# Layer 0 context attention: value products of all eight head pairs in one batch of four, in two PSUM banks

## The chip, the cores and the metric
The kernel is a four-layer network (a perceiver-like stack of cross attention, self attention and feed-forward blocks) written out by hand for one core of one Trainium2 chip. The metric is the device time of one execution in microseconds. Engines are named by their part: TensorE (PE in the rows, PEld for its weight loads), VectorE (DVE), ScalarE (ACT), GpSimd (POOL) and SyncE (SP), which issues the DMAs here.

## The reference, cut to what matters
Only the cross attention of layer 0 is touched. The input x has 128 batches of 32 rows of 128; the context has 257 rows of 256 for each batch. There are 16 heads of 64, and one learned null key and value beside the 257 of the context.

```python
def _L0_xattn_ref(x, context, Wq, Wkv, null_kv, Wout, ln_scale, ln_bias):
    HEADS, DH = 16, 64
    q = _split_heads(jnp.einsum('bnd,df->bnf', x, Wq)) * DH ** (-0.5)
    k, v = jnp.split(jnp.einsum('bmc,cf->bmf', context, Wkv), 2, axis=-1)
    ...                      # split into heads, the null key and value put in front
    attn = jax.nn.softmax(jnp.einsum('bhid,bhjd->bhij', q, k), axis=-1)
    out = jnp.einsum('bhij,bhjd->bhid', attn, v)
    out = jnp.einsum('bnf,fd->bnd', out.transpose(0, 2, 1, 3).reshape(b, -1, 1024), Wout)
    ...                      # layer norm with ln_scale and ln_bias
```

## The kernel before, in words
The kernel never forms keys and values. It multiplies the queries by the key weights (so that they stand in the 256 context channels), takes scores against the raw context, multiplies the probabilities by the raw context, and only then applies the value weights and the output weights.

The stage is `context_attention` (L3673). It works on 128 batches. Four batches make a tile (32 tiles of 4 x 32 = 128 rows). All its work is written out in one order for each engine, and the engines meet through counting semaphores. In the step of one batch n, at position b % 4 = 0, 1, 2 or 3 of its tile m, TensorE does in this order:

- `scores` (L3897): 16 matmuls of 257 columns into the four banks psA. It waits for `q_ready`, which both engines give when they have copied the queries out of psA (on VectorE L4084, on ScalarE L4036).
- `context` of the batch before (L3918): 128 matmuls into the four banks psB. It waits, among other things, for the transposed probabilities (`turned`, L4128) and for `values_read`, the count of value copies out of psB, since it writes those banks again.
- `fill` (L3881): 16 matmuls that make, in psA, the queries of the batch four later. Their copies are what the next `scores` waits for.
- `head_values` (L3929), at positions 1 and 3 only: the value weights applied to the finished contexts (`ot`) of the tile before. One call does four of the eight head pairs: 32 matmuls (four pairs, two halves of the context channels, two heads of a pair) into the one bank psB[:, 1]. VectorE copies the bank to `vo` (L4098) at the end of its own step.
- `output` (L3940, L3941), at position 0 only: 9 matmuls of the output weights with `vo`, for the tile two back, into psB[:, 2].
- `heads` (L3872): 4 matmuls for the queries of the next tile, into psB[:, 0], copied by ScalarE (L4042).

VectorE's step is: two maxima over the scores (L4105) with small follow-ups, the sum of the exponentials (L4117), its reciprocal, the copies of two context banks (L4090) and of two query banks (L4084), the scaling (L4123), the transpose (L4128), and at positions 1 and 3 the value copy (L4098). ScalarE does the exponentials (L4022) and the other copies. The first tile has no value products (there is no tile before it); the last tile has no `fill` and no `heads`, and its own values are computed behind the loop, in two banks of psA (L3929, 64 matmuls in one run). Each step of SyncE fetches one batch of the context in rows, and every second one two batches of it transposed, each behind a semaphore of its own; POOL copies the tail columns (L3837) and spreads them once a tile (L3846).

Which banks hold values when is told by `values_before`: it gives the count of value copies that `context` at position b must find done.

Of the kernel before, what the change touches and what calls it, by code (L numbers as in the profile page):

```python
# [26 lines left out]
BT = P // S  # L27
# [3645 lines left out]
def context_attention(k, w, w256_dram, nv_dram, queries_loaded):  # L3673
# [17 lines left out]
    with ctx:  # L3691
# [24 lines left out]
        psB = ps("c_psB", [P, G, CHUNK])  # L3716
# [24 lines left out]
        ot_ready = {e: k.sem(f"c_ot_ready_{e}") for e in ("act", "dve")}  # L3741
# [12 lines left out]
        def values_before(m, b, first):  # L3754

            if first and b < BT + 2:
                return None
            return 2 * (m - 1) + (b % BT) // 2

        with nc.Block() as block:  # L3760
            @block.sync
# [106 lines left out]
            def _(pe):  # L3868
# [7 lines left out]
                def fill(banks, j):  # L3876

                    for half in range(2):
                        for a in range(2):
                            for e in range(2):  # L3880
                                mm = pe.matmul(banks[:, 2 * a + e, half * P:(half + 1) * P],  # L3881
                                               w["k"][e * DV:(e + 1) * DV, 2 * j + a, half * P:(half + 1) * P],
                                               qh[e * DV:(e + 1) * DV, 2 * j + a], start=True, stop=True)
                    mm.then_inc(q_in, 1)

                def scores(i, b, first, last):
                    n = i * NB + b
                    for e in ("act", "dve"):
                        pe.wait_ge(q_ready[e], fills_before(i, b, last))
                    if b % 2 == 0:  # L3890
                        pe.wait_ge(kc_loaded[b // 2 % 2], (i * 2 + b // 4 + 1) * 32)
                    if not (first and b == 0):
                        pe.wait_ge(exp_done, n * EX)
                    pe.nop(nofuse=True)
                    for r in range(G):
                        for half in range(2):
                            mm = pe.matmul(psA[:, r, 0:KEYS],  # L3897
                                           qt[:, b // BT, half * BT + b % BT, r * G:(r + 1) * G].rearrange("p h i -> p (h i)"),
                                           kc[:, b // 2 % 2, b % 2, half], start=(half == 0), stop=(half == 1))
                        if r % 2:  # L3900
                            mm.then_inc(scores_done, 1)

                def context(n, b, count, valued, heads_read, outs_read, opening=False):

                    pe.wait_ge(turned, n + 1)
                    pe.wait_ge(vc_loaded[b % 4], count * 64)
                    pe.wait_ge(heads_ready, heads_read)
                    if valued is not None:
                        pe.wait_ge(values_read, valued)
                    if outs_read is not None:  # L3910
                        pe.wait_ge(out_read, outs_read)
                    if not opening:
                        pe.wait_ge(ot_ready["dve"], n)
                    pe.nop(nofuse=True)
                    for half in range(2):
                        for t in range(KB):
                            for e in range(G):
                                mm = pe.matmul(psB[:, e, half * P:(half + 1) * P],  # L3918
                                               vc[e * S:(e + 1) * S, b % 4, t, half * P:(half + 1) * P],
                                               pt[e * S:(e + 1) * S, :, t], start=(t == 0), stop=(t == KB - 1))  # L3920
                    mm.then_inc(context_done, 1)

                def head_values(bank, s, j):

                    for a in range(4):
                        for half in range(2):
                            for e in range(2):
                                h = (4 * j + a) * 2 + e
                                mm = pe.matmul(bank[e * DV:(e + 1) * DV, a * P:(a + 1) * P], wv[:, half, h],  # L3929
                                               ot[:, s, half * G + h // G, h % G].rearrange("p b i -> p (b i)"),  # L3930
                                               start=(half == 0), stop=(half == 1))
                    mm.then_inc(values_in, 1)

                def output(m, s):
                    pe.wait_ge(values_read, (m + 1) * 2)
                    pe.wait_ge(lz_ready, m + 1)
                    pe.wait_ge(wn_loaded[s], (m - s) * 32 + 64)
                    pe.nop(nofuse=True)
                    for p in range(H16 // 2):
                        pe.matmul(psB[:, 2, 0:D], vo[:, p], wo[:, p], start=(p == 0), stop=False)  # L3940
                    pe.matmul(psB[:, 2, 0:D], lz[:, s].rearrange("p b i -> p (b i)"), wn[:, s], start=False, stop=True)\  # L3941
                        .then_inc(out_done, 1)

                def chunk(i, first, last):
                    for b in range(NB):
                        n = i * NB + b
                        m, s = i * 2 + b // BT, b // BT
                        scores(i, b, first, last)
                        if not (first and b == 0):
                            c = (b - 1) % NB  # L3950
                            context(n - 1, c, i * 2 + (b - 1) // 4 + 1,
                                    values_before(m, b, first),
                                    min(n + 2, FILLS - FIRST + 1) if last else n + 2,
                                    m - 1 if b % BT == 1 and not first else None, first and b == 1)
                        if not (last and s == 1):
                            pe.wait_ge(heads_ready, n + 2)
                            pe.wait_ge(exp_done, n * EX + G)
                            pe.nop(nofuse=True)
                            fill(psA, b % BT)
                        if not (first and b == 0):  # L3960
                            pe.wait_ge(ot_ready["act"], n)
                        if b % 2 and not (first and s == 0):
                            if b % BT == 1:
                                pe.wait_ge(ot_ready["dve"], n)
                            pe.nop(nofuse=True)
                            head_values(psB[:, 1], 1 - s, b % BT // 2)
                        if b % BT == 0 and not first:
                            pe.wait_ge(ot_ready["dve"], n)
                            output(m - 2, s)
                        if not (last and (s == 1 or b == BT - 1)):  # L3970
                            to = (b + 1) % BT
                            pe.nop(nofuse=True)
                            heads(psB[:, 0], i * 2 + (b + 1) // BT + 1, (2 * to, 2 * to + 1))
# [107 lines left out]
            def _(v):  # L4081
# [11 lines left out]
                def take_values(bank, f, m, j, opening=False):  # L4093

                    v.wait_ge(values_in, f + 1)
                    if j == 0 and not opening:
                        v.wait_ge(out_done, m)
                    v.tensor_copy(vo[:, 4 * j:4 * j + 4].rearrange("p a t -> p (a t)"), bank)\  # L4098
                        .then_inc(values_read, 1)
# [38 lines left out]
                def chunk(i, first, last):  # L4138
                    for b in range(NB):
                        n = i * NB + b  # L4140
                        m, s = i * 2 + b // BT, b // BT
                        maxima(i, b)
                        if b % BT == 0 and not (first and b == 0):
                            turn_tail(m - 1, 1 - s)
                        invert(n, b)
                        if not (first and b == 0):
                            take_contexts(n - 1, (b - 1) % NB)
                        if not (last and s == 1):
                            take_queries(psA, n + FIRST, 1 - s, b % BT)
                        scale_and_turn(n, b, first)  # L4150
                        if b % 2 and not (first and s == 0):
                            take_values(psB[:, 1], 2 * (m - 1) + b % BT // 2, m - 1, b % BT // 2, first)
                        if b % BT == 2 and not first:
                            count_out(m - 2)

# [468 lines left out]
```

## Time and profile before

| | |
|---|---|
| median of 3 runs | 4436.02 us (4431.32 to 4437.11) |
| the profiled execution, its own time | 4436.19 us |
| its span in the trace | 4434.4 us, 116039 instructions |
| mean granted TensorE clock | 0.925 of full speed |
| busy shares of the span | TensorE 84%, VectorE 64%, ScalarE 45%, GpSimd 18% |
| the stage in question | about 94 to 1451 us of the span |

The span begins with the first instruction and ends with the last. A row of the timeline gives the start of a run of equal instructions, its length, the engine, the line, what it writes and reads, the shape and the count; idle time before it stands in square brackets with what ended it. The times of TensorE rows are those of pipelined matmuls: neighbouring rows overlap a little, so distances between starts are what is to be read.

### The profile page before, as it was taken

What the parts mean: (1) busy time and instruction counts of PE and PEld (TensorE: products, weight loads), DVE (VectorE), ACT (ScalarE), POOL (GpSimd) and SP (SyncE); (2) the same over time, 40 slices, a digit from 0 to 9 for tenths busy, and PEclk for the clock granted to TensorE, in tenths of its full rate; (3) what the DMA queues carried; (4) which work ended last, traced back from release to release, by engine and by line L of the source; (5) the groups of instructions that cost most, each with busy time, mean ns of one, the idle gap of its engine ahead of it and who ended that gap; (6) DMA issues with size and microseconds to landing.
All of it is one profiled execution on the core that took longest, in us unless ns stands there. A gap on an engine that the chain in (4) does not pass through costs nothing. (4 is left out here: it accounts for less than half of the span.)

```text
span 4434.4 us, 116039 instructions
## 1 busy us (share of the span) xinstructions
PE 3739.3 (84%) x46470; PEld 2858.7 (64%) x46470; DVE 2832.7 (64%) x5367; ACT 1998.2 (45%) x4327; POOL 818.1 (18%) x797
## 2 busy tenths in 40 slices
PE   5999999999999770499998689899996777879776
PEld 4888888888888440366765356566664345656454
DVE  3766767676766685522224867477777946878683
ACT  2333333333332555444343334488888745644323
POOL 0000000000000141100000056455552022200160
PEclk7999999999999885799999889899998889989878
DMA  5655656565564155400000033122220000000000
GB/s 134 131 128 129 129 123 129 128 129 124 128 129 93 42 160 160 158 1 0 0 0 26 21 117 151 68 68 69 68 69 18 0 6 3 0 13 0 9 2 25
DMA packets 307726, 320.09 MB, mean 72 GB/s; under 512 B 43440, under 2 KB 295248, under 8 KB 299872
## 3 DMA queue, kind: packets, MB, share of 16 engines
q1 hardware_dynamic: 307296, 313.84, 27.9%
q8 instruction: 333, 5.46, 0.5%
q14 instruction: 97, 0.79, 0.1%
HBM read 286.44 MB, written 27.05 MB: 71 GB/s over the span
## 5 line engine op out<-in xcount | busy, mean ns | idle before, releaser
L3897 PE MATMUL c_psA<-c_kc,c_qt 128*128 128x257 f32 x2048 | 470.7, 382 | 35.0 <-issue 27.1
L3918 PEld LDWEIGHTS c_psB<-c_pt,c_vc 32*128 32x128 f32 x16384 | 469.1, 187 | 43.9 <-issue 43.9
L3918 PE MATMUL c_psB<-c_pt,c_vc 32*128 32x128 f32 x16384 | 493.5, 273 | 1.3 <-DVE c_vo L4098 1.3
L3897 PEld LDWEIGHTS c_psA<-c_kc,c_qt 128*128 128x128 f32 x2048 | 379.7, 190 | 91.4 <-issue 41.3
L4022 ACT ACTIVATE c_sc<-c_psA,c_mx 128x257 f32<-128x257 f32 x512 | 215.4, 473 | 467.7 <-DVE c_mx L4109 467.7
L637 PEld LDWEIGHTS f_psY<-f_w_down,f_hT 128*128 128x128 f32 x2560 | 302.7, 192 | 64.3 <-issue 48.4
L680 ACT ACTIVATE f_hT<-f_psH,f_b_up 128x512 f32<-128x512 f32 x320 | 214.0, 688 | 278.1 <-PE f_psH L627 273.4
L637 PE MATMUL f_psY<-f_w_down,f_hT 128*128 128x128 f32 x2560 | 306.9, 276 | 9.7 <-ACT f_hT L680 5.3
L627 PE MATMUL f_psH<-f_xs,f_w_up 128*128 128x512 f32 x640 | 300.5, 605 | 17.2 <-ACT f_hT L680 17.2
L2320 POOL TENSOR_TENSOR x_sc<-x_sc,x_rec 128x1156 f32<-128x1156 f32 x128 | 270.7, 2115 | 208.4 <-DVE x_rec L2586 208.4
L743 DVE SCALAR_TENSOR_TENSOR X<-f_psY,f_wt,X 128x128 f32<-128x128 f32 x256 | 72.2, 344 | 364.3 <-PE f_psY L637 364.3
L4105 DVE TENSOR_REDUCE c_nm<-c_psA 128x2 f32<-128x514 f32 x256 | 176.6, 690 | 189.0 <-PE c_psA L3897 188.9
L2514 ACT ACTIVATE x_sc<-x_psS,x_mx 128x289 f32<-128x289 f32 x512 | 250.0, 501 | 75.8 <-DVE x_mx L2563 75.8
L3837 POOL COPY c_z<-c_sc 128x8 f32<-128x8 f32 x128 | 24.7, 193 | 1233.9 <-DVE c_sc L4123 1233.9
L2392 PE MATMUL x_psT<-ident,x_sc 128*128 128x128 f32 (+1 forms) x1536 | 216.8, 277 | 18.6 <-DVE x_pt L2570 12.1
L2563 DVE TENSOR_REDUCE x_mx<-x_psS 128x2 f32<-128x578 f32 x256 | 182.3, 753 | 77.5 <-PE x_psS L2377 77.5
L4117 DVE TENSOR_REDUCE c_sm<-c_sc 128x4 f32<-128x1032 f32 x128 | 157.2, 1228 | 99.7 <-ACT c_sc L4025 99.7
L2392 PEld LDWEIGHTS x_psT<-ident,x_sc 128*128 128x128 f32 (+1 forms) x1536 | 159.3, 131 | 87.6 <-issue 87.4
L627 PEld LDWEIGHTS f_psH<-f_xs,f_w_up 128*128 128x128 f32 x640 | 114.4, 193 | 127.7 <-issue 94.6
L4333 POOL TENSOR_TENSOR g_hT<-g_gate,g_wide 128x512 f32<-128x512 f32 x128 | 173.5, 1365 | 111.8 <-ACT g_gate L4423 89.7
L4030 ACT ACTIVATE c_ot<-c_psB 128x512 f32<-128x512 f32 x128 | 76.5, 597 | 243.0 <-PE c_psB L3918 243.0
L4359 PEld LDWEIGHTS g_psY<-g_w_down,g_hT 128*128 128x128 f32 x1024 | 132.5, 192 | 61.4 <-issue 39.2
(823 smaller groups left out, 7670.8 us busy)
## 6 DMA issues: line engine op xcount, KB each, us to landing
c_vc<-in_ctx SPq DMA_DIRECT2D x512, 256.0 KB
c_kc<-in_ctxT SPq DMA_DIRECT2D x128, 257.0 KB
g_wide<-g_w_dram SPq DMA_DIRECT2D x32, 1024.0 KB, 8.0
x_kc<-in_ctxT SPq DMA_DIRECT2D x32, 512.0 KB
x_vc<-in_ctx SPq DMA_DIRECT2D x64, 256.0 KB
l_k_dram<-l_dist SPq DMA_DIRECT2D x32, 256.0 KB, 4.2
l_q_dram<-l_turn SPq DMA_DIRECT2D x8, 1024.0 KB, 10.1
y_pt<-l_q_dram SPq DMA_DIRECT2D x8, 1024.0 KB, 6.8
```

Source lines behind the costliest of these rows:

```text
L627: pe.matmul(psH[:, n % BANKS, :], w_up[:, n, :], xs[:, b, :], start=True, stop=True).then_inc(up_done, 1)
L637: mm = pe.matmul(psY[:, e % YB, t * P:(t + 1) * P], hT[:, n % SLOTS, t * P:(t + 1) * P], w_down[:, n, :], start=(u == 0), stop=(u == UT - 1))
L680: act.activation(hT[:, n % SLOTS, :], psH[:, n % BANKS, :], ACT.Gelu, bias=b_up[:, n:n + 1]).then_inc(act_done, 1)
L2320: g.tensor_tensor(sc[:, slot], sc[:, slot], bcast(rec[:, slot], 2, NK), ALU.mult).then_inc(scaled, 1)
L2392: mm = pe.transpose(psT[0:width, bank, r * P:(r + 1) * P], sc[:, c % SC, r, t * P:t * P + width], k.ident[:])
L2514: act.activation(sc[:, b % SC, r], psS[:, r, 0:NK], ACT.Exp, bias=mx[:, b % 2, r:r + 1], accum_out=sm[:, b % SC, r:r + 1]).then_inc(exp_do ...
L2563: v.tensor_reduce(two, psS[:, half * 2:half * 2 + 2, 0:NK], AX, ALU.max, negate=True)\
L3897: mm = pe.matmul(psA[:, r, 0:KEYS], qt[:, b // BT, half * BT + b % BT, r * G:(r + 1) * G].rearrange("p h i -> p (h i)"), kc[:, b // 2 % 2, ...
L3918: mm = pe.matmul(psB[:, e, half * P:(half + 1) * P], vc[e * S:(e + 1) * S, b % 4, t, half * P:(half + 1) * P], pt[e * S:(e + 1) * S, :, t] ...
L4022: act.activation(sc[:, b % 2, r, 0:KEYS], psA[:, r, 0:KEYS], ACT.Exp, bias=mx[:, b % 2, r:r + 1]).then_inc(exp_done, 1)
L4105: v.tensor_reduce(nm[:, b % 2, two * 2:two * 2 + 2], psA[:, two * 2:two * 2 + 2, 0:KEYS], AX, ALU.max, negate=True).then_inc(reduced, 1)
L4333: g.tensor_tensor(hT[:, n % SLOTS], gate[:, n % SLOTS], wide[:, c % 2, e], ALU.mult)\
```

## The change
The value products of positions 1 and 3 both go to position 1: 64 matmuls, pairs 0 to 3 into psB[:, 1] as before and pairs 4 to 7 into psB[:, 3]. VectorE copies both banks at the end of its step of position 1. At position 3 nothing of this is left on either engine; the wait of position 1 for VectorE's context copies, which free bank 3, was there before. `values_before` now asks for both copies from position 2 on.

```diff
@@ values_before
             if first and b < BT + 2:
                 return None
-            return 2 * (m - 1) + (b % BT) // 2
+            return 2 * (m - 1) + (2 if b % BT >= 2 else 0)
@@ block.tensor, chunk
-                        if b % 2 and not (first and s == 0):
-                            if b % BT == 1:
-                                pe.wait_ge(ot_ready["dve"], n)
+                        if b % BT == 1 and not (first and s == 0):
+                            pe.wait_ge(ot_ready["dve"], n)
                             pe.nop(nofuse=True)
-                            head_values(psB[:, 1], 1 - s, b % BT // 2)
+                            head_values(psB[:, 1], 1 - s, 0)
+                            head_values(psB[:, 3], 1 - s, 1)
@@ block.vector, chunk
-                        if b % 2 and not (first and s == 0):
-                            take_values(psB[:, 1], 2 * (m - 1) + b % BT // 2, m - 1, b % BT // 2, first)
+                        if b % BT == 1 and not (first and s == 0):
+                            for j in range(2):
+                                take_values(psB[:, 1 + 2 * j], 2 * (m - 1) + j, m - 1, j, first)
```

## Rows read from the trace of the kernel before

**Rows 1.** The page: busy time, share of the span and instructions of each engine.
```profile
PE 3739.3 (84%) x46470; PEld 2858.7 (64%) x46470; DVE 2832.7 (64%) x5367; ACT 1998.2 (45%) x4327; POOL 818.1 (18%) x797
```

**Rows 2.** Busy time of the stage: window, length, engines, granted clock, DMA share, GB/s.
```profile
108.00:1442.00 1334.00, 1321.63 (x23361) 1184.18 (x23354) 932.28 (x1515) 430.34 (x1036) 37.02 (x159) 1.00 0.58 125
```

**Rows 3.** Waits from 150 to 1400 us: who waited for whom, us in total, times, longest.
```profile
PEld c_psA L3897 <- issue: 11.0, 31, 0.4
PEld c_psB L3872 <- issue: 10.1, 59, 0.2
PE c_psA L3897 <- DVE c_qt L4084: 5.9, 30, 0.2
```

**Rows 4.** Timeline of TensorE's matmuls, one tile: the scores that open each step.
```profile
690.18 3.64 PE L3897 MATMUL c_psA<-c_kc,c_qt 128*128 128x257 f32 x16
...
701.07 3.64 PE L3897 MATMUL c_psA<-c_kc,c_qt 128*128 128x257 f32 x16
...
710.42 3.71 PE L3897 MATMUL c_psA<-c_kc,c_qt 128*128 128x257 f32 x16 [0.20 <-DVE c_qt L4084]
...
721.39 3.64 PE L3897 MATMUL c_psA<-c_kc,c_qt 128*128 128x257 f32 x16
...
732.39 3.64 PE L3897 MATMUL c_psA<-c_kc,c_qt 128*128 128x257 f32 x16
```

**Rows 5.** Timeline, all engines, ends of the steps at positions 2 and 3.
```profile
708.42 0.97 PEld L3881 LDWEIGHTS c_psA<-c_qh,c_wk 64*128 64x128 f32 x16
...
709.51 0.52 PEld L3872 LDWEIGHTS c_psB<-XT,c_wq 128*128 128x128 f32 x4
...
709.63 0.69 DVE L4084 COPY c_qt<-c_psA 128x512 f32<-128x512 f32 x1 [0.38 <-PE c_psA L3881]
...
710.39 3.34 PEld L3897 LDWEIGHTS c_psA<-c_kc,c_qt 128*128 128x128 f32 x16 [0.36 <-issue]
...
718.94 1.73 PEld L3929 LDWEIGHTS c_psB<-c_ot,c_wv 128*64 128x64 f32 x32
...
719.06 0.69 DVE L4084 COPY c_qt<-c_psA 128x512 f32<-128x512 f32 x1 [0.38 <-PE c_psA L3881]
...
720.84 0.52 PEld L3872 LDWEIGHTS c_psB<-XT,c_wq 128*128 128x128 f32 x4 [0.17 <-issue]
```

**Rows 6.** Timeline of the first tile, where no step has value products: two opening scores.
```profile
122.32 3.71 PE L3897 MATMUL c_psA<-c_kc,c_qt 128*128 128x257 f32 x16 [0.20 <-DVE c_qt L4084]
...
131.75 3.71 PE L3897 MATMUL c_psA<-c_kc,c_qt 128*128 128x257 f32 x16 [0.20 <-DVE c_qt L4084]
```

**Rows 7.** Timeline, VectorE and the contexts' weight loads, from position 1 to 2.
```profile
700.60 1.25 DVE L4128 STREAM_TRANSPOSE c_pt<-c_sc 128x1024 f32<-128x1024 f32 x1
...
701.77 0.65 DVE L4098 COPY c_vo<-c_psB 128x512 f32<-128x512 f32 x1
703.01 0.69 DVE L4105 TENSOR_REDUCE c_nm<-c_psA 128x2 f32<-128x514 f32 x1 [0.58 <-PE c_psA L3897]
...
704.64 3.66 PEld L3918 LDWEIGHTS c_psB<-c_pt,c_vc 32*128 32x128 f32 x128 [0.33 <-issue]
```

**Rows 8.** The value products by their line in the whole trace: count, ns min/median/max.
```profile
L3929 PE MATMUL c_psB<-c_ot,c_wv x1984: 272/273/324, 149.7 to 1435.4; 128*64 128x128 f32 x199
```

**Rows 9.** Timeline of the last two tiles and of what follows the loop.
```profile
1394.64 0.69 DVE L4084 COPY c_qt<-c_psA 128x512 f32<-128x512 f32 x1 [0.38 <-PE c_psA L3881]
...
1396.42 3.34 PEld L3897 LDWEIGHTS c_psA<-c_kc,c_qt 128*128 128x128 f32 x16 [0.17 <-issue]
...
1434.83 1.25 DVE L4128 STREAM_TRANSPOSE c_pt<-c_sc 128x1024 f32<-128x1024 f32 x1
...
1436.00 0.65 DVE L4098 COPY c_vo<-c_psB 128x512 f32<-128x512 f32 x1
1436.98 3.69 PEld L3918 LDWEIGHTS c_psB<-c_pt,c_vc 32*128 32x128 f32 x128 [1.55 <-issue]
...
1444.00 3.47 PEld L3929 LDWEIGHTS c_psA<-c_ot,c_wv 128*64 128x64 f32 x64
```

## The prediction
> **What bounds the kernel now.** I read the page's busy shares first: TensorE 84% of the span, VectorE 64% [rows 1]. Such a share is a mean over stages, so the second view is the busy time of this stage alone: from 108 to 1442 us TensorE is busy for 1321.63 of 1334 us, 99%, at a granted clock of 1.00 (2.4 GHz), against 932 us on VectorE and 430 us on ScalarE, with the DMA engines at a share of 0.58 [rows 2]. Nothing else is near its limit, so the stage lasts as long as TensorE's stream, plus the places where that stream stops. The third view, the waits, shows how few these are: the scores' weight loads stood idle 31 times, 11.0 us in all, and 30 of these show as a wait for VectorE's query copy; the loads of `heads` stood idle 59 times for 10.1 us [rows 3]. No wait of TensorE on a DMA is among its waits there. The fourth view is the timeline of one tile, and it gives all the prices.
>
> Distances between the scores that open each step [rows 4]: position 1 takes 701.07 - 690.18 = 10.89 us, position 2 takes 710.42 - 701.07 = 9.35, position 3 takes 721.39 - 710.42 = 10.97, position 0 takes 732.39 - 721.39 = 11.00. The sum is 42.21 us a tile. Position 2, the only one with neither value products nor output, is also the only one behind which the scores stand idle for the query copy. The reader is to see why in [rows 5]: `fill` ends its loads at 708.42 + 0.97 = 709.39; the copy out of psA starts at 709.63 and lasts 0.69, to 710.32; the scores may load at 710.39. Between, TensorE has only the four loads of `heads`, from 709.51 to 710.03, so it idles 0.36. At position 3 the same copy starts at 719.06, 0.12 behind the value products' first load, and is done at 719.75, while TensorE has work until beyond 721: the value products hide it.
>
> **The change part by part.** The work is the same: 64 value matmuls a tile, two copies, no other shape. Only its place moves.
>
> *Position 1 gets 32 more matmuls.* They stand behind the first 32 with nothing between. Behind the loop 64 of them run in one go and their loads take 3.47 us [rows 9], where 32 take 1.73 [rows 5]; so the second 32 cost 3.47 - 1.73 = +1.74. All of it is on TensorE, which is the bound, and the copy of the queries was already hidden there: +1.74.
>
> *Position 3 loses 32.* They take 720.84 - 718.94 = 1.90 from their first load to that of `heads`, of which 0.17 is idle time ahead of `heads` [rows 5]. If nothing were late behind them, -1.90 would be the gain. But what is late next is the query copy, exactly as at position 2. A step that starts stalled and ends stalled is in the trace already: 131.75 - 122.32 = 9.43 us in the first tile, where there are no value products [rows 6]. So position 3 goes from 10.97 to 9.43: -1.54.
>
> *Position 0 then starts stalled.* Its scores' weights are no longer loaded beneath the matmuls ahead. The price is the difference between position 3 (stalled start, 10.97) and position 1 (10.89), which do the same work [rows 4]: +0.07 to +0.08, taken as 0.07 with the rounding of the starts.
>
> Sum for one tile: 1.74 - 1.54 + 0.07 = +0.27 to 0.28 us, taken as 0.275.
>
> *How often.* 1984 matmuls of L3929 write psB [rows 8], 64 for each of 31 tiles (1 to 31). The last two of these go another way, so the plain case counts 29 times: 29 x 0.275 = +8.0 us.
>
> *Tile 30.* Its position 3 has no `heads`, and the next scores load at 1396.42. The query copy ends at 1394.64 + 0.69 = 1395.33, and by the 0.07 of [rows 5] the scores could load at 1395.40 [rows 9]. So it gives 1.02 back for the 1.74 of position 1: +0.7.
>
> *Tile 31.* No `fill` and no `heads`. Position 1 pays its +1.74. At position 3 the value copy of VectorE (1436.00 + 0.65 = 1436.65) comes between the transpose (ends 1434.83 + 1.25 = 1436.08) and the last contexts, which load 0.33 later, at 1436.98 [rows 9]. Without it they start 0.33 behind the transpose, at 1436.41: -0.57. Together +1.2.
>
> *VectorE* gets a second copy of 0.65 at position 1 and loses one at position 3. The cover: today the copy at 701.77 ends at 702.42, and the maximum waits another 0.58 for the scores [rows 7]. The scores move back by 1.74 with everything on TensorE, so the first maximum comes at 704.75, and two copies end near 703.1: 1.6 us to spare. If that cover were gone, up to 0.65 a tile would go down the chain maximum, exponential, sum. The second copy also must not start before the second 32 products end: they load from 698.6 to 702.1 (3.47), and VectorE reaches the copy at about 702.4. The contexts at position 2 now wait for both copies; their loads start today at 704.64, by then at 706.4, 3.3 us behind the copies. Behind that waiting instruction stand `fill` and `heads`, but nothing waits. The wait for VectorE's context copies at position 1 is there already and costs nothing today: position 1 with it is no longer than position 3 without it [rows 4].
>
> *SyncE, POOL, ScalarE* issue what they did, in their old order. Positions 1 and 3 drift by 1.7 us against each other, against a DMA share of 0.58 [rows 2], and fetches run at least two steps ahead: nothing. The granted clock is at its upper level throughout [rows 2] and the gaps stay under half a microsecond: nothing.
>
> Total: 8.0 + 0.7 + 1.2 = +9.9 us. The bounds of each term: the stall at position 3 can be as small as none (then -1.90 and no 0.07, see rival A) and, beyond the copy, hardly larger, since [rows 6] repeats for every step of the first tile and [rows 5] gives the same start of the copy (0.38 idle ahead) at both positions. The 1.74 lies between 32 x 54 ns = 1.73 and the 1.90 with a gap of its own: at most +0.16 x 31 = 5 us more.
>
> The sum is made against the profiled execution's own time, 4436.19 us, 1.8 us over its span, and 0.17 over the median of 4436.02. So 4436.2 + 9.9 = 4446.1 us, +0.22%.
>
> **A rule of the Trainium skill.** The rows show 0.17 us idle ahead of `heads` when it follows the value products, and 0.12 (709.51 - 709.39) when it follows `fill` [rows 5]. The page "TensorEngine Tiling (Array Packing)", section Tiling Modes, Key Properties, says that changing the tiling mode drains the TensorE, while tiles of one mode run on independently. That would make the regrouping a gain, since each tile enters and leaves the 64-column tiling of the value products once less; the trace agrees that a switch has a gap, and 0.17 is already within my 1.90. By the rule alone the change would win, and that is the case A.
>
> **The rivals.**
> A. *Not slower: the query copy is not late.* If at position 3 the scores start as soon as `heads` is through, the matmuls only move, and each tile saves one gap of 0.17: 31 x 0.17 = -5.3 us, 4431 us (-0.12%). It decides by whether the copy ends (710.32 in its place of [rows 5]) before TensorE has run out of work (710.03). It speaks for it that the DVE step of position 3 no longer carries a value copy; against it, that this copy stands behind the query copy in VectorE's order, and that all of position 2's steps show the stall (30 of them in [rows 3]). Chance 0.07.
> B. *VectorE becomes late at position 2.* Two copies delay the maximum, and the exponentials hold `fill`: up to 0.65 x 30 = 20 us more, 4466 us. For: contexts start only 0.33 behind something that the trace doesn't name [rows 7]. Against: the 1.6 us above. Chance 0.04.
> C. *The 64 matmuls don't run on as one*: a gap of about 0.16 between the two banks, +5 us, 4451 us. For: the increment of `values_in` sits on the 32nd, and a new bank begins. Against: the 3.47 for 64 of [rows 9] also contains a bank change and that increment. Chance 0.06.
> D. *The change lies below what can be told*: something I don't see (fetching of instructions, the spacing of the DMAs) gives back a few us, 4436 to 4441. Chance 0.08. The same with the opposite sign is in the range's upper part.
>
> **How the numbers follow.** The forecast holds 0.75: slower by 9.9 us, its own range 4442 to 4450, since a median of three moves by some 2 to 3 us (4431.32 to 4437.11 in the runs before). A difference within 0.2% (8.9 us) is about what a measurement of this kernel can't tell from none, and 9.9 stands just above it: within the forecast I give 0.68 to its being over, 0.32 to its being under. Slower: 0.75 x 0.68 + 0.04 + 0.05 = 0.60. Faster by over 0.2%: only beyond case A, 0.03. Same: 0.37. The range takes in most of D and all of C: 4439 to 4452.
>
> **What would show it.** In the changed trace: L3929 in runs of 64 with loads of about 3.47 us at position 1, none at position 3; about 60 waits of the scores' loads of 0.36 us in place of 31; distances of the scores of about 12.6, 9.35, 9.43 and 11.07 us, 42.5 a tile; idle waits ahead of `heads` about 30 in place of 59; the last contexts waiting for the transpose. The prediction is wrong if position 3 takes less than 9.4 us, if position 1 takes more than 12.7, or if position 2's maximum shows no idle time before it.

## The result and the profile after

| | before | after |
|---|---|---|
| median | 4436.57 us (6 runs, 4428.04 to 4444.51) | 4456.07 us (6 runs, 4452.3 to 4458.41) |
| span of the profiled execution | 4434.4 us | 4456.4 us |

The ratio is 1.0047, with a 95% interval of 1.0031 to 1.0063: slower by 19.5 us between the medians, where 9.9 was forecast. 4456.07 lies 4 us outside the stated range, on the side that was forecast.

The page of the kernel after, first the busy times as in [rows 1], then its queue of instruction fetches (packets, MB, share of 16 engines), which I had not looked at before:

```profile
PE 3759.2 (84%) x46470; PEld 2875.3 (65%) x46470; DVE 2830.2 (64%) x5367; ACT 1998.3 (45%) x4327; POOL 817.7 (18%) x797
...
q8 instruction: 333, 5.46, 0.5%
```

TensorE does as many instructions as before and is busy 20 us longer; in the matmuls' pipelined records much of a wait hides as length. VectorE is busy 2.5 us less. So the answer must lie in TensorE's order of time. The rows count records, and a matmul of the code leaves two (16 matmuls of one `head_values` call are the 32 of a row, the 9 of `output` are 18); the counts of 64 and 128 below are such records too. This is one tile of the timeline of its matmuls, the counterpart of [rows 4]:

```profile
744.21 3.64 PE L3897 MATMUL c_psA<-c_kc,c_qt 128*128 128x257 f32 x16
...
752.65 3.71 PE L3929 MATMUL c_psB<-c_ot,c_wv 128*64 128x128 f32 x64
...
756.84 3.64 PE L3897 MATMUL c_psA<-c_kc,c_qt 128*128 128x257 f32 x16
...
766.20 3.71 PE L3897 MATMUL c_psA<-c_kc,c_qt 128*128 128x257 f32 x16 [0.20 <-DVE c_qt L4084]
...
775.63 3.71 PE L3897 MATMUL c_psA<-c_kc,c_qt 128*128 128x257 f32 x16 [0.20 <-DVE c_qt L4084]
...
786.70 3.64 PE L3897 MATMUL c_psA<-c_kc,c_qt 128*128 128x257 f32 x16
```

The distances of the scores are 12.63, 9.36, 9.43 and 11.07 us for positions 1, 2, 3 and 0: 42.49 a tile against 42.21. The prediction had 12.63, 9.35, 9.43 and 11.07. The waits of the weight loads from 150 to 1400 us, the counterpart of [rows 3], agree: 58 stalls ahead of the scores in place of 31, 30 gaps ahead of `heads` in place of 59.

```profile
PEld c_psB L3918 <- issue: 41.8, 123, 0.7
PEld c_psA L3897 <- issue: 20.9, 58, 0.4
PEld c_psB L3872 <- issue: 5.1, 30, 0.2
```

The first of these lines is what is new. The contexts' loads (L3918) waited 123 times in 117 steps, and up to 0.7 us. In the trace before, the same line shows one wait a step, of 0.3 us at most:

```profile
PEld c_psB L3918 <- issue: 39.3, 118, 0.3
```

Some runs of 128 equal matmuls, which have no wait between them, are broken in two; these places are called breaks here. This is the timeline of the weight loads in tiles 6, 14 and 22 (position 0):

```profile
351.70 3.20 PEld L3918 LDWEIGHTS c_psB<-c_pt,c_vc 32*128 32x128 f32 x109 [0.33 <-issue]
355.46 0.74 PEld L3918 LDWEIGHTS c_psB<-c_pt,c_vc 32*128 32x128 f32 x19 [0.56 <-issue]
...
693.01 2.98 PEld L3918 LDWEIGHTS c_psB<-c_pt,c_vc 32*128 32x128 f32 x101 [0.33 <-issue]
696.52 0.97 PEld L3918 LDWEIGHTS c_psB<-c_pt,c_vc 32*128 32x128 f32 x27 [0.53 <-issue]
...
1034.81 2.76 PEld L3918 LDWEIGHTS c_psB<-c_pt,c_vc 32*128 32x128 f32 x93 [0.33 <-issue]
1038.27 1.19 PEld L3918 LDWEIGHTS c_psB<-c_pt,c_vc 32*128 32x128 f32 x35 [0.71 <-issue]
```

The first row's 0.33 is the usual one ahead of the contexts [rows 7]; the second is the break. Summing how far each step of the plain tiles lies above the usual one of its position gives 6.0 us for the kernel after, of which 4.8 at position 0 and 1.3 at position 3, and one more of 0.45 in tile 30. The trace before had 0.3.

The other new thing is at the end of the loop. Weight loads of the last contexts, then the windows ahead of and inside them (window, length, busy times, granted clock, DMA share, GB/s), the counterpart of [rows 9]:

```profile
1457.57 6.57 PEld L3918 LDWEIGHTS c_psB<-c_pt,c_vc 32*128 32x128 f32 x128 [3.44 <-issue]
```
```profile
1454.00:1457.50 3.50, 0.32 (x12) 0.12 (x6) 3.08 (x3) 0.60 (x1) 0.19 (x1) 0.91 0.00 0
1457.60:1461.00 3.40, 3.40 (x64) 3.40 (x68) 0.00 (x0) 0.00 (x0) 0.00 (x0) 0.50 0.00 0
```

TensorE's weight loads stood idle for 3.44 us, with a granted clock of 0.91 in the window 1454.0 to 1457.5, and TensorE then ran the contexts at 0.50, that is at 1.2 GHz. They took 6.57 us where [rows 9] has 3.69.

The 22 us of the two spans come out so. Plain tiles, 29 x 0.29 = 8.4. Tile 30, its steps compared one by one and its break left out, +0.9. Tile 31: position 1 +1.75; from its last scores to the output products 18.47 us against 16.42, +2.05. Breaks +6.2. Before the first steps of the loop and in the first two of them +4.3, which belongs to the execution and not to the change: the first scores came at 96.31 us against 93.85, and the second execution of the changed kernel (below) reaches them at 91.01 us, before both. TensorE's granted clock from 49 to 60 us was 0.50 in the first trace after, 0.60 in the second and 0.66 in the trace before; so the clock may be a part of it, but doesn't put the three in order. That makes 23.6, and the stages behind took 1.6 less.

The breaks have a counterpart among the DMA packets. These are, for tile 22, a window ahead of the break and one inside it (columns as in [rows 2]), and the packets from 1035.3 to 1035.5 us (queue, packets, MB, share of 16 engines):

```profile
1030.50:1035.00 4.50, 4.30 (x24) 3.42 (x27) 3.77 (x6) 1.43 (x4) 0.19 (x1) 1.00 1.06 213
1037.60:1038.20 0.60, 0.16 (x5) 0.00 (x0) 0.57 (x2) 0.00 (x0) 0.00 (x0) 1.00 0.00 0
```
```profile
q1 hardware_dynamic: 31, 0.03, 82.7%
q8 instruction: 1, 0.02, 43.5%
```

The data loads filled the DMA engines for some 5 us. A packet of the instruction queue began as they ran out, at 1035.39, and was through at 1036.78. The matmuls went on at 1038.27, 1.49 us behind it, while no data moved at all.

### The profile page after: what moved, and what is told of

The parts are those of the page before. It is cut to its first block and busy times, and to the rows that moved or that the text cites. A ratio compares the mean times of both kernels' runs of the same rounds, so it can differ in the third digit from the quotient of the medians.

```text
span 4456.4 us, 116038 instructions
## 1 busy us (share of the span) xinstructions
PE 3759.2 (84%) x46470; PEld 2875.3 (65%) x46470; DVE 2830.2 (64%) x5367; ACT 1998.3 (45%) x4327; POOL 817.7 (18%) x797
## 3 DMA queue, kind: packets, MB, share of 16 engines
q8 instruction: 333, 5.46, 0.5%
## 5 line engine op out<-in xcount | busy, mean ns | idle before, releaser
L3918 PEld LDWEIGHTS c_psB<-c_pt,c_vc 32*128 32x128 f32 x16384 | 474.9, 188 | 49.2 <-issue 48.9
L3918 PE MATMUL c_psB<-c_pt,c_vc 32*128 32x128 f32 x16384 | 500.9, 274 | 5.1 <-DVE c_pt L4128 3.3
```

The source lines that it names most:

```text
L3918: mm = pe.matmul(psB[:, e, half * P:(half + 1) * P], vc[e * S:(e + 1) * S, b % 4, t, half * P:(half + 1) * P], pt[e * S:(e + 1) * S, :, t] ...
```

## The experiments

The two theories at the start: **T**, the 19.5 us are the stall that was forecast, more in the last tile than was forecast, and the breaks. **N**, the breaks are the chance of one execution.

### The same two kernels once more

No edit.

> The kernel before once more, as a kernel of its own. It tells how far one and the same program moves between executions and traces: ratio 1.000 within 0.2%. Theory T (the 20 us of the change are real and made of: 8.0 us for 29 tiles by the stall behind the query copy, some 4.6 us in the last two tiles, and 6 us of short stalls inside the contexts' matmuls): the trace shows again almost none of the short stalls (0.3 us above the regular step lengths in the trace before), steps of 10.89, 9.35, 10.97 and 11.00 us. Rival N (the short stalls are chance of one execution): they differ from trace to trace, this one may have several us of them.

Measured: 4431.91 us, ratio 1.000 (0.999 to 1.001). Steps of 10.89, 9.35, 10.96 and 11.00 us, and 0.34 us above them, in the same two steps and with the same sizes (0.16 and 0.18) as in the first trace.

> The changed kernel once more. Theory T: 4456 us, ratio to before 1.0045 (1.003 to 1.006); steps of 12.63, 9.35, 9.43 and 11.07 us, and again 4 to 9 us of short stalls, nearly all inside the contexts' matmuls at position 0. Rival N: the short stalls are gone or elsewhere, and the time is 4450 or lower.

Measured: 4458.16 us, ratio 1.005 (1.0033 to 1.0067). Steps of 12.64, 9.35, 9.43 and 11.08 us and 5.9 us of breaks, with 0.7 more in tile 30. The break of tile 22 is at the same matmul, behind 93 of the 128, and of the same length:

```profile
1029.19 2.76 PEld L3918 LDWEIGHTS c_psB<-c_pt,c_vc 32*128 32x128 f32 x93 [0.33 <-issue]
1032.65 1.19 PEld L3918 LDWEIGHTS c_psB<-c_pt,c_vc 32*128 32x128 f32 x35 [0.70 <-issue]
```

N is out: of the 12 steps that lie more than 0.04 us above the usual in the first trace, 11 do so in the second, among 15. Chance has a part in the sizes: tile 6 lost 0.83 us in the first trace and 0.31 in the second. The place is fixed by the program: from tile 6 to 14 to 22 it moves by 8 matmuls each time (109, 101, 93). Something that repeats nearly every eight tiles, but not with the tile, is a count of instructions; TensorE's code in this stage is unrolled, while the other engines run a loop. The instruction queue moves 5.46 MB in 333 packets, 16.4 KB each, so the program comes in blocks of fixed size. That a break is a block that comes late is the reading that the next experiments test.

### Both calls at position 3

```diff
-                        if b % BT == 1 and not (first and s == 0):
+                        if b % BT == 3 and not (first and s == 0):
                             pe.wait_ge(ot_ready["dve"], n)
...                      # take_values likewise; values_before gives 2 * (m - 1) throughout
```

> Both calls of the value products at position 3 instead of position 1 (banks 1 and 3 as in the change). Theory T: the regular part is the same, since two bare positions (1 and 2) stall for the query copy: steps of about 9.35, 9.43, 12.7 and 11.0 us, 42.48 a tile, +8 us. The short stalls follow the run of short steps: they move to the contexts at positions 2 and 3 and stay at some us in total. The last tile: the last contexts wait for two value copies, about +1.5 us against before, and TensorE does not idle for 3.4 us ahead of them, so its clock stays at the upper level. Total +12 to +18 us, 4449 to 4454. Rival P (position 1 is what costs, by the DVE's two copies ahead of the maximum or by the banks): position 1 free of them, nearly no loss, 4436 to 4440.

Measured: 4446.41 us, ratio 1.0028 (1.0016 to 1.0040), so 12 us slower than before, between 7 and 18. The scores that open the steps at positions 2, 3, 0 and 1, in the matmul timeline:

```profile
701.70 3.71 PE L3897 MATMUL c_psA<-c_kc,c_qt 128*128 128x257 f32 x16 [0.20 <-DVE c_qt L4084]
711.13 3.71 PE L3897 MATMUL c_psA<-c_kc,c_qt 128*128 128x257 f32 x16 [0.20 <-DVE c_qt L4084]
724.56 3.64 PE L3897 MATMUL c_psA<-c_kc,c_qt 128*128 128x257 f32 x16
735.56 3.64 PE L3897 MATMUL c_psA<-c_kc,c_qt 128*128 128x257 f32 x16
```

9.43, 13.43 (this tile has a break; the median of the position is 12.71), 11.00, and 9.35 for position 1. The steps are as expected, so it doesn't matter at which position the products pile up, only how many positions are left bare (with nothing of TensorE's but `heads` between `fill` and the next scores): rival P is out. The breaks are 4.3 us: 3.2 at position 3, in the contexts that follow the two bare steps, and one of 1.06 at position 2, in tile 29. In the changed kernel the bare steps are 2 and 3 and the breaks mostly at position 0, again the contexts behind the two. In the last tile the contexts wait for two value copies, +1.55 us against before, and load at the full clock, as expected.

### The last tile as before

```diff
+                            tail = last and s == 1
...                      # where tail: four pairs at position 1, four at position 3, both in bank 1
```

> The changed kernel, but the last tile keeps four pairs at position 1 and four at position 3. Theory T: the last tile gives back 1.74 us at position 1, and at position 3 TensorE has the value products to do while it waits for the last transpose, so its clock stays at the upper level and the last contexts load in 3.7 us instead of 6.6. Together 3.8 us less than the changed kernel: 4452. Rival C (the clock falls there anyway, by its own course): the last contexts still take 6.6 us, and only 1 us comes back.

Measured: 4449.34 us, ratio 1.0034 (1.0019 to 1.0049). The median is 6.7 us below that of the kernel after, and 8.8 below `again_after`; the breaks are 5.2 us here. The executions of one kernel scatter too much to read a 3.8 from this, but the trace tells it. Position 1 of tile 31 takes 10.18 us in place of 11.93; from the last scores to the output products 16.43 in place of 18.47. The last contexts, and the windows ahead of and inside them:

```profile
1451.54 3.69 PEld L3920 LDWEIGHTS c_psB<-c_pt,c_vc 32*128 32x128 f32 x128 [1.55 <-issue]
```
```profile
1448.20:1451.50 3.30, 1.97 (x32) 1.75 (x32) 2.97 (x4) 0.00 (x0) 0.19 (x1) 1.00 0.00 0
1451.60:1455.00 3.40, 3.40 (x121) 3.40 (x125) 0.00 (x0) 0.00 (x0) 0.00 (x0) 1.00 0.03 5
```

A wait of the same kind has 1.97 us of value products in it, the clock stays at 1.00, and 121 matmuls go where 64 went. Rival C is out: it was the idle time that the change made.

### Less and more on the DMA engines

First the changed kernel with half of the bytes of the context's rows (the other half of each buffer keeps old rows, so its results are not those of the kernel):

```diff
+                    rows = KB if fresh else KB // 2
                     for e in range(G):
-                        sp.dma_start(vc[e * S:(e + 1) * S, slot],
-                                     k.a["ctx"][ds(n, 1), 0:2 * P]...
+                        sp.dma_start(vc[e * S:(e + 1) * S, slot, 0:rows],
+                                     k.a["ctx"][ds(n, 1), 0:rows * S]...
```

> The changed kernel, with every load of the context's rows after the first three cut to its first half (128 of 256 rows, as many DMAs; the other half of the buffer keeps old rows, so that part of the products is made of old data). Theory S (the short stalls are TensorE's instructions coming late, because the fetches share the DMA engines with the context loads): the stalls inside the contexts' matmuls go from about 6 us to under 1 us, and the steps stay at 12.64, 9.35, 9.43 and 11.08 us; time about 6 us under the changed kernel, 4450. Rival R (the stalls come from TensorE itself, its banks or its weight loads): they stay at 5 to 6 us, 4456.

Measured: 4447.53 us, ratio 1.0027 (1.0017 to 1.0038), and no step of a plain tile more than 0.04 us off its median of 12.64, 9.36, 9.43 and 11.08: the breaks are gone to the last. The waits of the weight loads:

```profile
PEld c_psB L3919 <- issue: 39.3, 118, 0.3
PEld c_psA L3898 <- issue: 21.2, 59, 0.4
PEld c_psB L3873 <- issue: 5.1, 30, 0.2
```

The stalls for the query copy stand as they were, 59 of them, and the contexts' line is back to that of the kernel before: 39.3 us in all, none above 0.3. This run also tests the sum. Without breaks the rest should be 8.4 + 0.9 + 3.8 = 13.1 us, and its median is 12.6 over that of before.

Then the kernel before with more bytes:

```diff
+        spare = sb("c_spare", [S, 4, KB // 2, C])
...
+                    if not fresh:
+                        sp.wait_ge(spare_loaded[slot], prior * 16)
+                    sp.dma_start(spare[:, slot],
+                                 k.a["ctx"][ds(n, 1), 0:P]...).then_inc(spare_loaded[slot], 16)
```

> The kernel before, with one more DMA of 128 KB a batch into a buffer that nobody reads: 1409 instead of 1281 KB a batch, which over a mean step of 10.55 us is what the changed kernel moves in its steps of 9.4 us. Theory S: short stalls inside the contexts' matmuls appear where the trace before had none: 2 to 10 us in all, 4439 to 4447. Rival R: none, steps unchanged, 4436 to 4437.

Measured: 4440.14 us, ratio 1.0006 (0.9997 to 1.0015): by the time alone it can't be told from no change. The trace tells it: steps as before (10.89, 9.36, 10.96, 11.00), and 2.6 us above them in seven steps, where both traces of before had 0.3 in two. The longest wait of the contexts' loads is 0.8 us; that one lies in tile 1 at position 1, behind the three bare steps of the first tile, costs 0.9 us and comes on top of the 2.6.

```profile
PEld c_psB L3926 <- issue: 41.4, 123, 0.8
PEld c_psA L3905 <- issue: 10.8, 30, 0.4
PEld c_psB L3880 <- issue: 10.1, 59, 0.2
```

All seven are at position 3, behind position 2, which is the short step of that kernel. So the breaks come and go with the data traffic, in both kernels, with the matmuls untouched: rival R is out. The traffic per batch is the same before and after the change, 1281 KB; what the change made is two short steps in a row, 140 GB/s over 18.8 us, where before a single short one stood between long ones.

That the late thing is a block of instructions is seen in the traces' packets. The six traces with breaks (`three_calls`, below, among them) have 35 of more than 0.1 us in the contexts' loads. Each of the 35 ends 1.2 to 1.6 us behind the end of a packet of the instruction queue, while these packets come 7.3 us apart on average; and in each the data loads had filled the DMA engines up to within 1 us of the packet's start. In `half_bytes` the packet ahead of that place in tile 22 was through at 1021.80 us, and TensorE came to the matmul behind the first 93 at 1028.36, 6.6 us later, with no break. A rival that no run was made for, that the loads slow TensorE's own reading, fails on the window inside the break above: nothing moved there. A full stretch ahead of a packet is common and mostly costs nothing; why it does at these places is read from the two short steps, and isn't shown for each.

### Three calls

The theory says what would be better than either: no bare step at all.

```diff
+    PARTS = ((0, 3), (3, 6), (6, 8))
-            return 2 * (m - 1) + (b % BT) // 2
+            return 3 * (m - 1) + max(b % BT - 1, 0)
...
-                        if b % 2 and not (first and s == 0):
+                        if b % BT and not (first and s == 0):
...
-                            head_values(psB[:, 1], 1 - s, b % BT // 2)
+                            head_values(psB[:, 1], 1 - s, b % BT - 1)
...                      # copies and counts likewise, three a tile
```

> From the kernel before: the value products in three calls, pairs 0 to 2 at position 1, 3 to 5 at position 2, 6 and 7 at position 3, all in bank 1 with a copy each. Theory T: every step of a tile then has work behind the fill that hides the query copy. A bare step with the stall hidden is 10.89 - 1.90 = 8.99 us; three pairs add 24 x 0.054 + 0.17 = 1.47, two pairs 1.04: steps of 10.46, 10.46, 10.03 and 11.00 us, 41.95 a tile in place of 42.21, 29 x 0.26 = 7.6 us less; some 1 us lost in the last tile; no short stalls above 1 us. 4429 to 4431, ratio 0.9985. Rival V (the third copy and wait on VectorE make it late): steps of positions 2 and 3 longer than that, no gain, 4436 or more.

Measured: 4429.18 us, ratio 0.9986 (0.9973 to 0.9999). Steps of 10.46, 10.45, 10.02 and 11.00 us, 41.93 a tile, and 0.2 us of breaks, with 0.3 more in tile 1. The waits of the weight loads:

```profile
PEld c_psB L3919 <- issue: 39.9, 120, 0.3
PEld c_psB L3873 <- issue: 15.2, 89, 0.2
PEld c_psA L3898 <- issue: 0.2, 1, 0.2
```

One stall ahead of the scores is left of 31 and 58, for 30 more gaps of 0.17 ahead of `heads`. It is the fastest of the kernels here, though by little: the interval just excludes no change. Its steps give 7.8 + 0.3 us in tiles 1 to 30 and lose 1.0 in tile 31; the medians show 5.7. Rival V is out: the shorter copies of VectorE hold nobody.

## Why the prediction was too low

- **The plain tile** was right: 12.63, 9.36, 9.43 and 11.07 us as forecast, +0.29 a tile in place of 0.275; 8.4 us in place of 8.0. The moved matmuls cost 1.74, the query copy is what is late next at position 3, and position 0 starts stalled. `three_calls` shows the same mechanism from the other side.
- **Tile 30** was right: +0.9 for +0.7. Its position 3 gave 0.88 back and not 1.02.
- **Tile 31** was wrong at its position 3. I had seen that the contexts would no longer wait for the value copy, and taken off 0.57; they did start 0.83 us earlier, only 0.07 behind the transpose. But I had written that the gaps stay under half a microsecond and the clock therefore stays, which is read from plain tiles; [rows 9] already shows 1.55 in the last one. Taking work out from under a wait leaves the wait as idle time, here 3.44 us, and the contexts behind it then ran at 0.50: +2.88. The step gave +2.05 in place of -0.57. Every term of a removed cover has to be followed to the clock as well as to the next wait.
- **"SyncE, POOL, ScalarE ... nothing"** was the step that failed most, 6 us. The drift of the steps was put against a mean DMA share of 0.58, and against data that is fetched two steps ahead. Data did come in time: no wait on a DMA is among TensorE's waits after either. TensorE's own instructions did not: their packets began late, behind stretches in which the loads filled the DMA engines, which the mean of 0.58 hides, and the matmuls went on 1.2 to 1.6 us behind each packet. They are in no wait of the kernel's code. The page had them, in a line with a share of 0.5%.
- **The rivals.** A, the query copy not late, is refuted by 58 stalls. B, VectorE late at position 2: the maximum there now waits 1.68 us for the scores in place of 0.58, close to the 1.6 forecast, and `half_bytes`, with the same copies, has no loss there. C, a gap between the two banks: the 64 matmuls run as one. D expected a few us from "fetching of instructions, the spacing of the DMAs"; the place was right, the likelier sign was not.
- **The size.** 8.4 + 0.9 + 3.8 + 6.2 = 19.3 us of change in the traces, against 19.5 between the medians. That they agree so closely is luck, since the ratio's interval runs from 14 to 28 us. My own range of the likeliest case, 4442 to 4450, had taken run-to-run scatter for the only unknown.

On the instructions the Trainium skill has a rule: "Runtime: NRT & Kernel Launch", section Instruction fetch mechanics, says that each engine's instructions come in blocks of 16 KiB through a DMA queue of its own, and calls the fetch hidden by the pace of issue. The packets of 16.4 KB agree. That it is hidden doesn't hold for this case: the breaks in the runs of 128 matmuls last up to 0.7 us in the first trace, end behind such packets, and are gone in `half_bytes`.

## What to carry to other kernels

Count the places where an engine waits, not only the work: on an engine that is busy 99% of a stage, moving work from one place to another costs what the place left behind no longer hides, and the cheapest filler is one piece in each place that would stall. A long gap left on TensorE is paid twice if the clock falls. And where a long unrolled run of short matmuls stands beside steady loads, the spacing of the loads matters for the instructions too: look for runs of equal instructions that break with no wait between them, and lay the packets of the instruction queue beside them.

## What the runs showed of the hardware

- The same program breaks at the same matmul in two executions (behind 93 of 128 in tile 22), by 0.71 and 0.70 us; with half of the context bytes it doesn't break at all (77 GB/s over the stage), with 9% more traffic than before (140 against 128 GB/s) the old order breaks as well.
- In six traces each of 35 breaks ends 1.2 to 1.6 us behind the end of a 16.4 KB packet of the instruction queue. In tile 22 that packet began at 1035.39 us, when the loads had held the DMA engines at a share of 1.06 for 4.5 us.
- After 3.44 us of idle time the granted clock was 0.50, and 128 matmuls took 6.57 us of loads in place of 3.69. With 1.97 us of matmuls within 3.3 us the clock stayed at 1.00.
- Executions of the kernel before lay between 4427 and 4447 us. One part lies ahead of the loop: the changed kernel reached its first scores at 96.31 us in one execution and at 91.01 in another, with a granted clock of 0.50 and 0.60 from 49 to 60 us.
